# Four weight sets kept in split form: stored to device memory at the first use, loaded ready-made at the second

## The reference

```
x = x + 0.5 * L0_ffn(ln(x)); x = x + L0_attn(ln(x)); x = x + 0.5 * L0_ffn(ln(x))
x = x + 0.5 * L1_ffn(ln(x)); x = x + L1_attn(ln(x)); x = x + 0.5 * L1_ffn(ln(x))
x = x + 0.5 * L2_ffn(ln(x)); x = x + L2_attn(ln(x)); x = x + 0.5 * L2_ffn(ln(x))
x = x + 0.5 * L3_ffn(ln(x)); x = x + L3_attn(ln(x)); x = x + 0.5 * L3_ffn(ln(x))
```

## Time and profile before

| what | value |
|---|---|
| median of 3 runs | 3355.32 us |
| span of the profiled execution | 3352.4 us |
| median less span (what lies around it) | 2.9 us |
| PE, DVE, POOL, ACT busy | 86%, 67%, 51%, 44% |
| bytes moved by DMA | 221.68 MB, 66 GB/s over the span |
| starts T0 of the second L0, L1, L2, L3 | 1122.9, 1758.4, 2540.6, 3099.4 us |

### The profile page before, as it was taken

The page is one execution under the profiler, slowest core; times in us unless marked ns, Lnnn a source line. Parts: engine busy times, 40 slices in busy tenths (PEclk is TensorE's granted clock), DMA queues, the critical chain, the costliest instruction groups (busy, mean ns, idle before and its releaser), DMA issues. The chain is left out here.

```text
span 3352.4 us, 60248 instructions
## 1 busy us (share of the span) xinstructions
PE 2886.6 (86%) x21018; PEld 2571.8 (77%) x21018; DVE 2246.5 (67%) x5794; ACT 1489.5 (44%) x3235; POOL 1704.0 (51%) x1645
## 2 busy tenths in 40 slices
PE   8979999999999898876897968479996858976898
PEld 6869999999999787865686957367775847965687
DVE  6767777777777667755536666568886545655655
ACT  3255666666656424335323443344444334433342
POOL 2355556565656317444406356458886546340743
PEclk9989999999999899997898968779998869988899
DMA  2022221212121202230103434400002443330333
GB/s 72 1 74 70 54 70 54 71 54 70 54 70 54 69 1 82 75 103 27 37 0 98 125 99 118 114 18 2 2 2 70 125 119 85 114 99 0 95 103 97
DMA packets 129187, 221.68 MB, mean 66 GB/s; under 512 B 18609, under 2 KB 68145, under 8 KB 128881
## 3 DMA queue, kind: packets, MB, share of 16 engines
q1 hardware_dynamic: 95026, 147.47, 14.8%
q0 software_dynamic: 21216, 57.96, 6.7%
q10 hardware_dynamic: 12672, 12.58, 1.1%
HBM read 170.23 MB, written 47.72 MB: 65 GB/s over the span
## 5 line engine op out<-in xcount | busy, mean ns | idle before, releaser
L1632 POOL DMA_INDIRECT MXG<-dxn,IDX x250 | 237.3, 949 | 231.9 <-PE bank L1204 171.9
L1642 POOL DMA_INDIRECT YG<-dyo,POSI x192 | 187.3, 976 | 215.7 <-DMA dyo<-YS 112.5
L2519 POOL TENSOR_SCALAR SX<-SX,MN 128x256 f32<-128x256 f32 x256 | 233.7, 928 | 57.2 <-DVE MN L2443 57.1
L1615 POOL TENSOR_TENSOR MWL<-RAW,MWH 128x608 fp32r<-128x608 f32 (+2 forms) x118 | 181.2, 1543 | 43.2 <-ACT MWH L1307 37.0
L2443 DVE CUSTOM_DVE_ANT_0 SX<-bank,FMASK 128x128 f32<-128x128 f32 (+1 forms) x512 | 156.1, 351 | 51.5 <-PE bank L2333 51.4
L1026 POOL TENSOR_TENSOR HL<-HID,HH 128x512 fp32r<-128x512 f32 x56 | 72.4, 1294 | 223.9 <-ACT HH L993 223.4
L515 PE MATMUL bank<-MWH,GH 128*128 x500 | 173.8, 348 | 10.1 <-DVE HB L1555 4.7
L515 PE MATMUL bank<-MWH,SHH 128*128 128x256 f32 x352 | 111.7, 317 | 73.2 <-POOL SHL L1486 29.2
L1329 ACT ACTIVATE GH<-bank 128x256 fp32r<-128x256 f32 x250 | 96.7, 387 | 173.5 <-PE bank L1204 161.2
L1613 POOL CAST MWH<-RAW 128x608 fp32r<-128x608 f32 (+2 forms) x78 | 56.8, 728 | 220.6 <-DVE X L901 120.7
L517 PE MATMUL bank<-MWH,GL 128*128 x500 | 157.8, 316 | 0.0
(11 more groups left out here) (459 smaller groups left out, 11615.3 us busy)
## 6 DMA issues: line engine op xcount, KB each, us to landing
dyo<-YS SPq DMA_DIRECT2D x250, 128.0 KB
RAW<-in_wheads SPq DMA_DIRECT2D x68, 320.0 KB
RAW<-in_eL SPq DMA_DIRECT2D x64, 304.0 KB
BB<-dgates SPq DMA_DIRECT2D x68, 256.0 KB, 3.6
GB<-dgates SPq DMA_DIRECT2D x68, 256.0 KB, 4.3
dxn<-XN ACTq DMA_DIRECT2D x16, 512.0 KB
RAW<-in_eL SPq DMA_DIRECT2D x32, 256.0 KB
RAW<-in_sL SPq DMA_DIRECT2D x18, 384.0 KB
```

The costliest lines, as they stand in the source:

```text
L1615: nc.gpsimd.tensor_tensor(MWL[:, at_:at_ + cols], RAW[:, n % RAW_SLOTS, 0:cols], f32(MWH[:, at_:at_ + cols]), ALU.subtract).then_inc(w_rea ...
L1632: nc.gpsimd.indirect_dma_start(MXG[:, n % XGS, :], None, dxn, bass.IndirectOffsetOnAxis(ap=IDX[:, b:b + 1], axis=0)).then_inc(x_in[n % XGS ...
L1642: nc.gpsimd.indirect_dma_start(YG[:, i % YGS, :], None, dyo[0:m.blocks * P, :], bass.IndirectOffsetOnAxis(ap=POSI[:, c * NT + t:c * NT + t ...
L2519: nc.gpsimd.tensor_scalar(part, part, MN[:, n % RING2, 1:2], None, ALU.subtract).then_inc(s_less1, 1)
```

## The change

`dkept` is new memory on the device for the split weights of L0, L1, L2 and L3. At the first use of a layer (`keeps`) SP also stores each high and each low piece there; the last instruction of DVE in that stage waits until the stores have landed (`w_kept`). In L1, L2 and L3 the high pieces go behind the RAW load of the piece four later, the low pieces behind every second `dyo` store. At the second use (`cached`) POOL splits nothing and SP loads no RAW: it waits until `x_done` says that the stage before is complete, and then issues all loads at once, the shared pieces one by one (high and low), the experts of a mixture in eight DMAs of 2432 columns (2048 in L2). PE waits for `first_in`, `pieces_in` and `experts_in` in place of `w_ready`. The expert columns now begin at column 2304 in all three mixtures. The total width of a weight tile (14336 columns) is the same.

```diff
+EXPERT_COL, LAST_COL, SPLIT_AT = 2304, 14336, 3
-        self.base = J * self.cols
+        self.base = EXPERT_COL
+        self.shared_at = [LAST_COL - (J - j) * self.cols if j >= SPLIT_AT or not gated else j * self.cols for j in range(J)]
...
+        def piece_there(pe, st, j):
+            if st.cached:
+                others = st.others + (st.f.J if st.f else st.m.J) - 1
+                pe.wait_ge(pieces_in if j else first_in, 32 * (others if j else st.loads + 1))
+            else:
+                pe.wait_ge(w_ready, st.pieces + j + 1)
...
+                if st.keeps and t == NT - 1:
+                    dve.wait_ge(w_kept, 16 * (st.kept + 2 * st.m.pieces))
...
         def moe_pool(pool, st):
-            pieces_low(pool, st, 0, m.pieces if not st.tailed else min(m.J, 4))
+            if not st.cached:
+                pieces_low(pool, st, 0, m.pieces if not st.tailed else min(m.J, 4))
...
         def moe_sync(sp, st):
-            for j in range(m.pieces):
+            if st.cached:
+                moe_fill(sp, st)
+            for j in range(0 if st.cached else m.pieces):
...
+                if st.keeps and j >= RAW_SLOTS:
+                    keep_piece(sp, st, 0, j - RAW_SLOTS)
...
                 sp.dma_start(dyo[b * P:(b + 1) * P, :], YS[:, n % 3, :]).then_inc(y_out[n % 3], 16)
+                if st.keeps and b % 2 and b // 2 < m.pieces:
+                    keep_piece(sp, st, 1, b // 2)
...
+        def keep_piece(sp, st, low, j):
+            at_, cols = piece_of(st.m, j)
+            part = slice(at_, at_ + cols)
+            sp.dma_start(dkept[st.name][low, :, part], f32((MWL if low else MWH)[:, part])).then_inc(w_kept, 16)
+
+        def moe_fill(sp, st):
+            m = st.m
+            sp.wait_ge(w_kept, 16 * st.kept)
+            sp.wait_ge(x_done, st.xd)
+            for j in range(m.J):
+                part = slice(m.shared_at[j], m.shared_at[j] + m.cols)
+                sp.dma_start(f32(MWH[:, part]), dkept[st.name][0, :, part]).then_inc(pieces_in if j else first_in, 16)
+                sp.dma_start(f32(MWL[:, part]), dkept[st.name][1, :, part]).then_inc(pieces_in if j else first_in, 16)
+            wide = m.E * m.ecols * 2 // FILLS
+            for i in range(FILLS // 2):
+                part = slice(m.base + i * wide, m.base + (i + 1) * wide)
+                sp.dma_start(f32(MWH[:, part]), dkept[st.name][0, :, part]).then_inc(experts_in, 16)
+                sp.dma_start(f32(MWL[:, part]), dkept[st.name][1, :, part]).then_inc(experts_in, 16)
```

More of the change, by code:

```diff
@@ L125, in __init__ @@
         self.router = self.m.router if self.m else 0
+        self.keeps, self.cached = False, False
+        self.kept, self.loads, self.others, self.fills = 0, 0, 0, 0
         (self.pieces, self.steps, self.ln, self.tr, self.l0, self.moe, self.rt, self.added, self.blocks, self.xd, self.gates) = before
@@ L141 @@
 RAW_SLOTS, RAW_COLS = 4, 768
-MOEW = max(_m.width for _m in MOES.values())
+MOEW = LAST_COL
 MAXB = max(_m.blocks for _m in MOES.values())
@@ L397, in build @@
         dyo = nc.dram_tensor('dyo', [NBP * P, D], F32).ap()
+        dkept = {n: nc.dram_tensor('dkept' + n, [2, P, MOEW], F32).ap() for n in MOES}
+        dkept['L0'] = nc.dram_tensor('dkeptL0', [2, P, FFNW], F32).ap()
         def sem(name):
@@ L406, in build @@
         w_ready = sem('w_ready')
+        w_kept = sem('w_kept')
+        first_in, pieces_in, experts_in = sem('first_in'), sem('pieces_in'), sem('experts_in')
         x_done = sem('x_done')
@@ L454, in build @@
         gg_gate, os_done = sem('gg_gate'), sem('os_done')
-        stages = []
+        stages, kept, kept_all, loads, others, fills = [], {}, 0, 0, 0, 0
         pieces = steps = ln = tr = l0 = moe = rt = added = blocks = xd = gates = 0
@@ L464, in build @@
                 stages[-1].next = st
+            st.cached = name in kept
+            st.keeps = name in dkept and not st.cached
+            st.kept, st.loads, st.others, st.fills = kept_all, loads, others, fills
+            if st.keeps:
+                kept_all += 2 * (st.f.J if st.f else st.m.pieces)
+                kept[name] = kept_all
+            if st.cached:
+                st.kept = kept[name]
+                loads += 1
+                others += (st.f.J if st.f else st.m.J) - 1
+                fills += st.kind == 'moe'
             if kind == 'ffn':
-                pieces += st.f.J
+                pieces += 0 if st.cached else st.f.J
                 steps += NW * st.f.J
@@ L471, in build @@
             if kind == 'moe':
-                pieces += st.m.pieces
+                pieces += 0 if st.cached else st.m.pieces
                 steps += st.m.steps
@@ L1057, in added @@
                 dve.wait_ge(prod_done, EXPERTS * st.l0 + i + 1)
+                if st.keeps and i == EXPERTS - 1:
+                    dve.wait_ge(w_kept, 16 * (st.kept + 2 * st.f.J))
                 if j == L0_E:
@@ L1090, in l0_vector @@
                     product(EARLY_UPS + 3 + i)
+        FILLS = 8
         LOGIT, COUNT = 4, 5
@@ L1132, in shared_up @@
             if w == 0:
-                pe.wait_ge(w_ready, st.pieces + j + 1)
+                piece_there(pe, st, j)
             for u in range(m.ups):
                 for k in range(KC):
-                    col = j * m.cols + (u * KC + k) * P
+                    col = m.shared_at[j] + (u * KC + k) * P
                     last = mm3(bank[2 * u + s % 2][:, :], (MWH[:, col:col + P], MWL[:, col:col + P]), xt(k, w * W, W),
@@ L1241, in moe_tensor @@
             pe.wait_ge(routed, 4 * st.moe + 3)
-            pe.wait_ge(w_ready, st.pieces + m.pieces)
+            if st.cached:
+                pe.wait_ge(experts_in, 16 * FILLS * (st.fills + 1))
+            else:
+                pe.wait_ge(w_ready, st.pieces + m.pieces)
             cols = []
@@ L1295, in piece_of @@
         def piece_of(m, j):
-            return (j * m.cols, m.cols) if j < m.J else (m.base + (j - m.J) * m.piece, m.piece)
+            return (m.shared_at[j], m.cols) if j < m.J else (m.base + (j - m.J) * m.piece, m.piece)
         def pieces_by(m, s):
@@ L1655, in moe_sync @@
                     sp.dma_start(RAW[:, n % RAW_SLOTS, 0:m.piece], d['e' + st.name][j - m.J, :, :]).then_inc(raw_in[n % RAW_SLOTS], 16)
+                if st.keeps and j >= RAW_SLOTS:
+                    keep_piece(sp, st, 0, j - RAW_SLOTS)
+            if st.keeps:
+                sp.wait_ge(w_ready, st.pieces + m.pieces)
+                for j in range(m.pieces - RAW_SLOTS, m.pieces):
+                    keep_piece(sp, st, 0, j)
             for b in range(m.blocks):
@@ L1659, in moe_sync @@
                 sp.dma_start(dyo[b * P:(b + 1) * P, :], YS[:, n % 3, :]).then_inc(y_out[n % 3], 16)
+                if st.keeps and b % 2 and b // 2 < m.pieces:
+                    keep_piece(sp, st, 1, b // 2)
+            if st.keeps:
+                for j in range(m.blocks // 2, m.pieces):
+                    keep_piece(sp, st, 1, j)
+        def keep_piece(sp, st, low, j):
[15 more added lines that the diff above has]
+                sp.dma_start(f32(MWL[:, part]), dkept[st.name][1, :, part]).then_inc(experts_in, 16)
         def gates_tensor(pe, st, n):
@@ L2712, in load_pieces, with keep_ffn, ffn_fill @@
                 sp.dma_start(RAW[:, n % RAW_SLOTS, 0:cols], src[j, :, :]).then_inc(raw_in[n % RAW_SLOTS], 16)
+        def keep_ffn(sp, st):
+            for j in range(st.f.J):
+                part = slice(j * st.f.cols, (j + 1) * st.f.cols)
+                sp.wait_ge(w_ready, st.pieces + j + 1)
+                sp.dma_start(dkept[st.name][0, :, part], f32(WH[:, part])).then_inc(w_kept, 16)
+                sp.dma_start(dkept[st.name][1, :, part], f32(WL[:, part])).then_inc(w_kept, 16)
+        def ffn_fill(sp, st):
+            sp.wait_ge(w_kept, 16 * st.kept)
+            sp.wait_ge(x_done, st.xd)
+            for j in range(st.f.J):
+                part = slice(j * st.f.cols, (j + 1) * st.f.cols)
+                sp.dma_start(f32(WH[:, part]), dkept[st.name][0, :, part]).then_inc(pieces_in if j else first_in, 16)
+                sp.dma_start(f32(WL[:, part]), dkept[st.name][1, :, part]).then_inc(pieces_in if j else first_in, 16)
         @block.sync
@@ L2727, in _ @@
             for st in stages:
-                if st.kind == 'ffn':
+                if st.kind == 'ffn' and st.cached:
+                    ffn_fill(sp, st)
+                if st.kind == 'ffn' and not st.cached:
                     load_pieces(sp, st, d['w' + st.name], st.f.J, st.f.cols)
+                if st.kind == 'ffn' and st.keeps:
+                    keep_ffn(sp, st)
                 if st.kind == 'moe':
```

6 lines of the change are left out of this document (3 added, 3 removed).

## The result

The changed kernel takes 3372.16 us (median of 4 runs, 3371.31 to 3377.0) against 3353.22 us (4 runs) for the kernel before. The ratio is 1.0054, with a 95% interval from 1.0038 to 1.0071: slower by 18 us (19 between the two medians). The forecast was 3371. The total fits better than its parts; two of them are off by 4 to 8 us and cancel.

What follows compares the result with a forecast made beforehand. POOL's splitting was taken to draw out DVE, on the path at stage starts. Gains of 14.4 us against held-up dxn stores net +14.9; first uses +1 make +16 on 3355.3: 3371 us, range 3340 to 3396.

Steps and rivals of the forecast that it cites:

- DVE's long instructions come from POOL's splitting: Second uses: DVE instructions are drawn out while POOL splits, such as 172 ns in the median to 911 at worst.
- The gain: Second uses without splitting: L0 1.4, L1 3.4, L2 2.1, L3 7.5, together 14.4 us, if nothing new is late.
- the front of L1 and L3: From T0, when loads are issued, to the first read of the logits: 1.4 us shorter in each.
- the dxn stores wait for the fill: Second L1, L2, L3: stores land only when all is moved, delaying step 0; theory A, +16, 3371 us, chance 0.62.
- Landing: End of dxn stores in second L1, L2, L3: issue and landing 2.9 us, plus fill, plus the stores' own 6.3.
- Rival C: Second-use fills read slowly, at 270 GB/s, for their 57344-byte pitch: +58, 3413 us, chance 0.12.
- B: Second uses: engines give q10 several store rows per fill row, so stores are not held up: -13, 3342 us, chance 0.18.
- The one-for-one share: DMA engines alternate q1 and q10 by packets, at best one for one, so stores get about a tenth of the bytes.
- 2.9 + ..., and with 1.28 + 0.60: Before step 0 in second L2 and L3: 1.28 and 0.60 us added after landing; L3 product +12.6, L2 subtraction +2.8.
- what is given back behind step 0: Shorter DVE work after step 0 offsets the delay: 2.0 us in L1, 0.6 in L2, 4.7 in L3.
- low stores ... each may be a block late for nothing: First L2 and L3: low stores between dyo stores cost nothing, since YS has three slots and the gathers four.
- first uses +1 with bounds 0 and 5: Storing the split weights once at first use costs 1 us in all, bounds 0 and 5.

Runs made afterwards that it cites:

- experiment 2: Changed kernel with only first-use stores; second use loads RAW and splits as before: 1.0022 of the kernel before. Issuing expert fills behind dxn stores instead: 0.9959 of this.
- after_again: The changed kernel, unaltered, measured again on another chip: ratio 1.0046 to the kernel before.
- before_again: The kernel before, unaltered, run again for its profile on the chip of after_again, where it takes 3289.2 us.
- high_only: Changed kernel storing only the high pieces at the first use, second use splitting as before: ratio 1.0001 to the kernel before.
- narrow_rows: Changed kernel with expert fills in 32 DMAs (2432-byte rows in L1 and L3) in place of eight: 0.9971 of the kernel before, 0.9950 when measured again.

## Why the prediction came out

**Right: DVE's long instructions come from POOL's splitting.** In the changed kernel DMA moves more than before in the same stretches and POOL is idle, and the instructions are short. The gain, forecast at 14.4 us, measured 13.5, give or take 4.6 (experiment 2). In the front of L1 and L3 it was 1.1 us at an equal clock, forecast 1.4.

**Right: the dxn stores wait for the fill**, row for row, until all has been moved. Landing was forecast at T0 + 40.8, 33.4 and 46.8; the waits end at T0 + 39.3, 32.6 and 44.9. The term was 1.5, 0.8 and 1.9 us too large, in the main since the engines moved 412 GB/s (3.73 + 0.39 MB in 10 us) and not 390. Rival C (270 GB/s) fell with that, and B with the waits. The one-for-one share was read from the earlier trace rows, 248 packets to 94, and there it was partly luck: in those 2 us the last rows of the stores were running out (28, 35, 21 and 10 of q10 in the four half microseconds), so that window measures no share. The windows after do. Of the Trainium skill's rule (DMA: Bandwidth & Descriptors, Queues, rings and completion order: a whole packet, typically 9 to 17 descriptors, before the next queue) the runs show nothing; they show nearly equal numbers of rows from each queue in the windows above, in which both had work throughout, at rows of 9728, 4864 and 2432 bytes. Turns of several rows from each queue would give the same sums.

**Wrong by 1.3 us a stage: the table load stands before the wait.** "2.9 + ..., and with 1.28 + 0.60" put ACT's table load behind the landing. It ran ahead of it in all three stages. Step 0's product in L3 came 9.5 us later than before and not 12.6, its subtraction in L2 0.8 and not 2.8.

**Right in size: what is given back behind step 0.** L3: 9.5 down to 4.5 at the end, forecast 4.7. L1: 5.3 down to 3.5 at the first gather, forecast 2.0.

**Not forecast: 4 us more in the late shared steps of the second L1.** The gather stood at +3.5, the stage ended at +7.5. The chain goes over an idle stretch of ACT (its releaser given as remote) and the clock:

```profile
1939.33 0.60 ACT L1322 ACTIVATE SGS<-bank 128x512 f32<-128x512 f32 x1 [4.57 <-remote]
```

```profile
1943.39 0.55 PE L535 MATMUL bank<-MWH,SHH 128*128 128x256 f32 x1 [3.06 <-DVE X L1534]
```

```profile
1937.00:1942.00 5.00, 3.33 (x17) 2.50 (x16) 2.04 (x5) 1.72 (x3) 1.04 (x2) 1.00 0.18 52
1942.00:1947.00 5.00, 3.61 (x15) 3.45 (x16) 4.11 (x9) 0.63 (x1) 2.49 (x3) 0.54 0.13 34
```

The kernel before has such a stretch too, of 4.06 us, at 1931.29, and PE did not run dry over it; and while TensorE was at its lower level here from 1942.4 to 1949.2, in the kernel before it fell to it only 0.8 us before the end of the stage. In after_again, where the clock stayed up in the same place, the stage is 3.6 us longer than in before_again, the part that the wait explains. So the 4 us go with the single execution and not with the mechanism, as far as two pairs of profiles can say; what sets the place of that idle stretch stays open.

**Wrong: "low stores ... each may be a block late for nothing", first uses +1 with bounds 0 and 5.** The stores cost 7 us (4 to 11), by high_only all of it the low ones. I had taken the block as long enough to cover 0.31 MB for every second one. That fits L1, where 39 blocks follow at 1.9 us each and YS waits 1.5 us in all. In the first L2, 47 blocks follow at 1.5 us each (67.1 us for 46 steps in before_again) and DVE waits 4 to 5 us for `dyo` without any such stores; with them the blocks took 2 to 3 us more at an equal clock. Where the rest of the 7 us lies is not shown, and moving these stores gave no total that can be told from narrow_rows.

So +16 was -14.4 + 29.3 + 1, and what the runs show is about -13.5 + 21 to 25 + 7, each term give or take 4 to 5. The sum came out because the held-up stores were sized 4 to 8 us too large (the landing and the table load, 8.0 us in the three stages together) and the first uses 6 too small. The direction and the wait were foreseen; that the total fits to a microsecond or two is luck.

## What to carry to other kernels

When a transfer that nobody waits for is made large and early, look for small-row transfers on other queues that somebody does wait for: they get one row for one of its rows, so their time is set by the length of its rows and then by its end. Cut the large one into rows near the others' size, or issue it after them; either turned a loss of 0.5% into a gain of 0.2 to 0.5%. And before calling a store hidden, compare it with the period of the loop it goes into, in each stage, and look whether that loop already waits for its own stores, as the first L2 does here.

## What the runs showed of the hardware

- The share of a queue goes by the number of rows, not bytes: 430 to 378 at 9728 and 1024 bytes (9% of the bytes for the short ones), 777 to 736 at 4864 and 1024, 1295 to 1155 at 2432 and 1024 (29%).
- Reads of 9728-byte rows at a pitch of 57344 bytes ran, with the stores beside them, at 412 GB/s over ten microseconds and 418 and 423 over six; the kernel before had 381 over its busiest six (9.5 to 15.5).
- A DVE instruction of 170 ns took 900 beside POOL's splitting and stayed at 170 beside 418 GB/s of DMA with POOL idle.
- TensorE's granted clock in the front of one and the same stage of one kernel differs between two executions on two chips: 17.1 us at the lower level in one and 6.8 in the other, with the table load of step 0 at T0 + 33.3 and T0 + 28.7.
